# A state-space block and six layers of local attention and FFN: rounded output product, keys placed by transfer, Gelu from PSUM, new orders

## The chip, the cores and the metric

The kernel runs on one core of one Trainium2 chip. The metric is the device time of one execution in microseconds, median of three: 3040.13 us before the change (3039.28 to 3040.23). PE is TensorE, DVE is VectorE, ACT is ScalarE, POOL is GpSimd, SP is SyncE.

## The reference

Input x has 128 sequences of 32 tokens of 128 features. First comes a state-space block: input projection, a causal convolution of four taps, silu, a layer norm, and over the 32 tokens in order a recurrence of a state of 16 rows by 256 channels for each sequence, clipped to +/-10 at each step; the result is gated and projected back to 128 features.

```python
def step(h, inputs):
    ad, bd, xt, ct = inputs
    h = jnp.clip(h * ad[:, :, None] + bd[:, :, None] * xt[:, None, :], -10.0, 10.0)
    yt = jnp.einsum('bd,bdh->bh', ct, h)
    return (h, yt)
```

Then come six layers. Each shifts half of the features by one token, forms q, k, v (16 heads of 64) by a product of 128 by 3072, normalises and rotates q and k, attends with a causal mask within a window of 32 tokens (here one sequence), and adds the output product (1024 by 128) to the residual. An FFN follows: a token shift, layer norm, a product to two times 341, `a * gelu(gate)`, and a product back to 128, added to the residual. At the end x is added.

## The kernel before

Everything is written by hand: each engine has its own program, and semaphores order them. There are three parts.

**cond_block** handles the state-space block. A first loop over the 32 tokens convolves and normalises. In a second loop, the recurrence, ACT forms the outer products of the input with the state's coefficients in PSUM (outer), DVE updates state rows (recur, L518), POOL updates the rows below PS (side, one row) from ACT's product side_u, DVE clips all 16 rows (clip, L528), and PE sums the rows with diagonal matrices (y_product, L239) that POOL writes (diagonals, L436). PE's project first puts the bias into PSUM by a product with ones (L207). POOL's side waits for the clip of the step before, PE's y_product for the clip of its own step.

**stack** handles the six layers. Each layer has 32 tiles of 128 tokens in 8 groups of four, so there are 192 tiles and 48 groups in all. A body(i, l, g) on every engine has four steps j. In step j the engines work on tiles of several ages: tile n is projected, tile n-1 is transposed (transpose_q, transpose_k at L803, copy_qT, copy_kT), tile n-2 has its scores and exponentials, tile n-3 its values (weigh_values L855) and its output copy (copy_oT L1028). The order of calls within body is each engine's order of work and nothing else sets it. Layer 0's groups 0 and 1 are unrolled, the others of it, and all eight of each later layer, are in hardware loops (group_steps).

The projection (L775) is three rounded (float32r) passes for each half of 512 columns: w_hi with xs_hi, w_lo with xs_hi, w_hi with xs_lo, where hi is the rounded value and lo the rest. Each layer's weights come in eight parts (load_part on SP, into a w_part of two buffers), which ACT rounds (round_part, L1099) and POOL completes (rest_of_part, L1335) during the layer before. The two PSUM tiles pa hold q, k and v in turn. ACT squares q and k, DVE sums the squares (L1161) and multiplies by sines (L1177) and cosines (L1168), and POOL adds the two (rotate, L1312) and scales the keys (norm_keys, L1321). project_v waits for DVE's cosines of q, and the next project_q for those of k. The keys are copied on ACT in two pieces of 64 partitions (L1011) into the layout of kT, block by block. Probabilities are transposed by DVE (L1186) and placed into pT by four DMAs on SP's queue. The values' result px is copied to oT, which has two buffers by group:

```python
if k == 0:
    wait_for(act, s["wo_done"], g - 1)
act.copy(oT[:, bass.ds(g % 2, 1), :, k, :]...
```

The output product project_out (L868) is one fp32 product of 512 columns for each of eight head pairs, 16 instructions, in j=3 of the body behind the group, half before transpose_k and half after. add_attention (DVE, L1233) adds it to res. The FFN runs in the body after that: centre (L1070) and variance in j=0, normalise (DVE, L1226), scale_shift (ACT, L1091), three gate products (L894) in j=1 with a bias copy each (gate_bias, L1036), then one Gelu over all (L1043) between two table loads; three a products (L905), gated (L1218), and down (L912) in j=2.

**add_input** transposes the residual and adds x.

Of the kernel before, what the change touches and what calls it, by code (L numbers as in the profile page):

```python
# [15 lines left out]
F32 = mybir.dt.float32  # L16
# [6 lines left out]
P = 128  # L23
# [3 lines left out]
PS = 1  # L27
# [22 lines left out]
EXP_LN = "natural_log_exp_and_others"  # L50

# [11 lines left out]
def cond_block(nc, d, res, spare, w0_loaded):  # L63
    with ExitStack() as ctx:
# [3 lines left out]
        def sem(name):  # L68
# [19 lines left out]
        wx, wxdt = room[0:NPROJ, 6656:6912], room[0:DS, 6912:7168]  # L88
        ident = sb("c_ident", [P, P])
# [5 lines left out]
        ones = sb("c_ones", [P, P])  # L95
        dt_bias = sb("c_dt_bias", [32, NPROJ])
# [24 lines left out]
        side_u = sb("c_side_u", [P, 2, PS, DI])  # L121
# [6 lines left out]
        names = """win_loaded taps_loaded ln_loaded late_loaded bias_loaded zeroed winT_done winT_ready taps_ready tap_mul  # L128
            tap_bias_ready late_done late_ready var_ready x_transposed xT_ready conv_done gate_done pre_ready silu_done gate_ready
            stats_done aggr_done rstd_ready centred xn_ready sq_done clamped scale_ready dx_ready neg_a_tanh neg_a_ready  # L130
            xnT_done xnT_ready proj_done bc_ready dtt_ready decay_mul decay_ready side_u_ready side_mul side_ready
# [5 lines left out]
        with nc.Block() as block:  # L137
            @block.sync
            def _(sp):
                sp.dma_start(ident[:], d["ident"]).then_inc(s["win_loaded"], 16)  # L140
                sp.dma_start(win, d["W_in"].rearrange("(r p) m -> p r m", p=P)).then_inc(s["win_loaded"], 16)
                for k in range(S // XCHUNK):
# [6 lines left out]
                sp.wait_ge(s["zeroed"], 7)  # L149
                sp.dma_start(dt_bias[0:1, 2 * DS:NPROJ], d["b_dt"].rearrange("(o n) -> o n", o=1))\  # L150
                    .then_inc(s["bias_loaded"], 16)
# [6 lines left out]
            def _(pe):  # L158
# [42 lines left out]
                def project(t):  # L201
                    if t < S:
                        if t == 0:
                            pe.wait_ge(s["bias_loaded"], 16)
                        wait_for(pe, s["bc_ready"], t)
                        wait_for(pe, s["dtt_ready"], t)
                        pe.matmul(pproj[:, 0:NPROJ], ones[0:32, :], dt_bias[:], start=True, stop=False)  # L207
                        pe.wait_ge(s["xnT_ready"], t + 1)
                        for f in range(2):
                            last = pe.matmul(pproj[:, 0:NPROJ], xnT[:, f, :], proj_w[:, f, :], start=False, stop=(f == 1))  # L210
# [59 lines left out]
            def _(act):  # L270
# [6 lines left out]
                for tile, name, n in ((lng, "ln_g", DI), (lnb, "ln_b", DI), (dskip, "D", DI), (alog[:], "A_log", DS)):  # L277
                    act.dma_start(tile, row(name).to_broadcast([P, n])).then_inc(s["ln_loaded"], 16)
# [23 lines left out]
                def late_copies():  # L302
# [7 lines left out]
                    act.wait_ge(s["ln_loaded"], 4 * 16)  # L310
# [8 lines left out]
                def tanh_dt(t):  # L319
                    if t < S:  # L320
                        act.wait_ge(s["proj_done"], t + 1)
                        wait_for(act, s["decay_mul"], t - 1)
                        act.activation(dtt[:, t % 2, :], pproj[:, 2 * DS:NPROJ], ACT.Tanh).then_inc(s["dtt_ready"], 1)
# [38 lines left out]
                for t in range(S):  # L362
# [6 lines left out]
                    if t >= S - 3:  # L369
                        k = t - (S - 3)  # L370
                        copy_xnT(k)
                        if k:
                            tanh_dt(k - 1)
                square(S - 2)
                square(S - 1)
                side_outer(0)
                outer(0, 0, 2)
                for t in range(S + 3):
                    outer(t, 2, NPAIR)
# [1117 lines left out]
```

## Time and profile before

| what | value |
|---|---|
| median of three runs | 3040.13 us |
| the profiled execution | 3038.72 us |
| its span, first to last instruction | 3036.9 us |
| mean granted TensorE clock | 0.985 |
| PE busy, share of the span | 2893.9 us, 95% |
| DVE busy | 2400.4 us, 79% |
| ACT busy | 2425.5 us, 80% |
| POOL busy | 2079.6 us, 68% |
| recurrence | about 95 to 404 us |
| layers | about 408 to 3019 us |

In a timeline a row gives the start of an instruction, its duration, its engine, line, operation and tiles. Neighbours on one engine overlap by a little, so the distance of two starts is what an instruction takes from its queue, and its duration is what its follower on another engine sees. PE's ends are modelled.

### The profile page before, as it was taken

How to read it: one execution, taken by the hardware profiler on the slowest of the kernel's cores; microseconds unless marked ns; L12 is line 12 of the kernel's file. 1: busy time of each engine (PE TensorE's matmuls, PEld its weight loads, DVE VectorE, ACT ScalarE, POOL GpSimd, SP SyncE). 2: the span in 40 equal slices, each digit the busy share in tenths (PEclk: the TensorE clock that was granted, in tenths of full speed). 3: DMA queues.
4: the chain of work that ended last, by engine and by line, in shares of the span. 5: the costliest groups of instructions: out<-in, count | busy, mean ns of one | idle time of the engine just before them, and what ended most of it. 6: DMA issues, size and time to landing. Idle time of an engine off the chain costs nothing. (4 is left out here: it accounts for less than half of the span.)

```text
span 3036.9 us, 90328 instructions
## 1 busy us (share of the span) xinstructions
PE 2893.9 (95%) x35040; PEld 2002.2 (66%) x35040; DVE 2400.4 (79%) x3168; ACT 2425.5 (80%) x3783; POOL 2079.6 (68%) x1518
## 2 busy tenths in 40 slices
PE   8799978999999999999999999999999999999996
PEld 7688856666666666666666666666666666666662
DVE  7899967888788878778887787887788787888871
ACT  5788857888788888878788887878888887888872
POOL 6655557777777777677777677777777776776760
PEclk9899989999999999999999999999999999999997
DMA  1000011010011001010100110010110101100002
GB/s 51 22 1 1 1 28 29 23 26 23 23 32 34 23 20 26 24 38 23 26 23 22 33 31 25 21 26 24 28 33 23 26 23 26 28 21 21 18 20 64
DMA packets 72899, 76.58 MB, mean 25 GB/s; under 512 B 22937, under 2 KB 46551, under 8 KB 72663
## 3 DMA queue, kind: packets, MB, share of 16 engines
q1 hardware_dynamic: 71782, 74.01, 9.5%
q10 hardware_dynamic: 1008, 1.19, 0.2%
q8 instruction: 61, 1.00, 0.1%
q14 instruction: 48, 0.39, 0.0%
HBM read 22.71 MB, written 2.10 MB: 8 GB/s over the span
## 5 line engine op out<-in xcount | busy, mean ns | idle before, releaser
L1312 POOL TENSOR_TENSOR qk_r<-qk_r,qk_t 128x1024 f32<-128x1024 f32 x384 | 917.3, 2389 | 552.3 <-DVE qk_r L1168 388.0
L775 PE MATMUL pa<-w_hi,xs_hi 128*128 128x512 f32 x1152 | 577.1, 501 | 43.1 <-DVE qk_r L1168 26.1
L1161 DVE TENSOR_REDUCE ss<-sq 128x16 f32<-128x1024 f32 x384 | 463.5, 1207 | 18.7 <-ACT sq L958 18.4
L1177 DVE TENSOR_TENSOR qk_t<-pa,rot 128x1024 f32<-128x1024 f32 x384 | 465.4, 1212 | 0.0
L1168 DVE TENSOR_TENSOR qk_r<-pa,rot 128x1024 f32<-128x1024 f32 x384 | 465.3, 1212 | 0.0
L803 PEld LDWEIGHTS px<-ident_sb,qk_r 128*128 128x128 f32 x3072 | 350.9, 141 | 164.7 <-issue 100.4
L775 PE MATMUL pa<-w_hi,xs_lo 128*128 128x512 f32 x1152 | 455.8, 396 | 0.0
L775 PE MATMUL pa<-w_lo,xs_hi 128*128 128x512 f32 x1152 | 454.3, 394 | 0.0
L803 PE MATMUL px<-ident_sb,qk_r 128*128 128x128 f32 x3072 | 401.4, 274 | 30.7 <-POOL qk_r L1321 14.9
L1011 ACT COPY kT<-px 64x1024 f32<-64x1024 f32 x384 | 385.1, 1003 | 35.7 <-PE px L803 31.0
L1321 POOL TENSOR_TENSOR qk_r<-qk_r,inv 128x1024 f32<-128x1024 f32 x192 | 365.6, 1904 | 44.4 <-ACT inv L995 44.3
L775 PEld LDWEIGHTS pa<-w_hi,xs_hi 128*128 128x128 f32 x1152 | 217.6, 189 | 224.0 <-issue 178.0
L1186 DVE STREAM_TRANSPOSE prT<-pr 128x512 f32<-128x512 f32 x192 | 136.6, 711 | 265.6 <-POOL pr L1343 262.8
L868 PE MATMUL pg<-spare,wo 128*128 (+1 forms) x768 | 345.4, 592 | 1.1 <-ACT spare L1028 1.1
L965 ACT ACTIVATE sq<-pa 128x1024 f32<-128x1024 f32 x192 | 196.3, 1022 | 170.3 <-DVE ss L1161 160.3
L1028 ACT COPY spare<-px 128x1024 f32 (+1 forms) x192 | 193.2, 1006 | 108.9 <-PE px L855 107.8
L775 PEld LDWEIGHTS pa<-w_lo,xs_hi 128*128 128x128 f32 x1152 | 219.0, 190 | 78.3 <-issue 52.3
L775 PEld LDWEIGHTS pa<-w_hi,xs_lo 128*128 128x128 f32 x1152 | 217.7, 189 | 50.6 <-issue 0.2
L1343 POOL TENSOR_TENSOR pr<-pr,rden 128x512 f32<-128x512 f32 x192 | 201.8, 1051 | 66.6 <-DVE rden L1209 66.6
L239 PE MATMUL c_bank<-c_h,c_cdiag 128*128 128x256 f32 x1024 | 230.7, 384 | 10.9 <-DVE c_h L528 10.8
L868 PEld LDWEIGHTS pg<-spare,wo 128*128 128x128 f32 x768 | 141.9, 190 | 143.7 <-issue 138.4
L342 ACT ACTIVATE c_bank<-c_xn,c_bc 128x256 f32<-128x256 f32 x480 | 203.3, 468 | 38.4 <-DVE c_bc L504 24.2
(145 smaller groups left out, 5431.0 us busy)
## 6 DMA issues: line engine op xcount, KB each, us to landing
pT<-prT SPq DMA_DIRECT2D x768, 64.0 KB, 2.0
w_part<-in_Wqkv SPq DMA_DIRECT2D x40, 192.0 KB, 2.6
wo<-in_Wo SPq DMA_DIRECT2D x6, 512.0 KB, 4.1
c_h<-in_x SPq DMA_DIRECT2D x4, 512.0 KB, 9.0
o_x<-in_x SPq DMA_DIRECT2D x8, 256.0 KB, 5.1
out<-o_out SPq DMA_DIRECT2D x8, 256.0 KB, 4.3
w<-in_W SPq DMA_DIRECT2D x6, 341.0 KB
spare<-in_Wqkv SPq DMA_DIRECT2D x1, 1536.0 KB, 6.3
```

The lines of the kernel that those rows point to most:

```text
L239: last = pe.matmul(py[t % 2][:, 0:DI], cdiag[:, t % 3, n, :], h[:, t % 2, n, :], start=False, stop=(n == DS - 1))
L342: last = act.activation(pu[k % 2][:, (n - lo) * DI:(n - lo + 1) * DI], xn[:, t, :], ACT.Copy, scale=bc[:, t % 2, 0, n:n + 1])
L775: last = pe.matmul(pa[(u + c) % 2][:, half * 512:half * 512 + 512], x[:, j * P:(j + 1) * P], w[:, at], start=(k == 0), stop=(k == 2))
L803: last = pe.transpose(px[:, hp * P:(hp + 1) * P], qk_r[:, j % 2, c, hp * P:(hp + 1) * P], ident[:])
L868: last = pe.matmul(pg[:], wo[:, hp, :], heads_out, start=(hp == 0), stop=(hp == HP - 1))
L1011: act.copy(kT[rows, :, :, half, :].rearrange("p h b j -> p (h b) j"), px[rows, :].rearrange("p (h j) -> p h j", j=S)).then_inc(s["tk_out"], 1)
L1161: dve.reduce_sum(ss[:, c, :], heads(sq[:]), AX.X).then_inc(s[sum_sem], 1)
L1168: dve.tensor_tensor(heads(qk_r[:, j % 2, c, :]), heads(pa[(3 * j + c) % 2][:]), per_head(rot[:, l % 2, 2 * c, :]), ALU.mult).then_inc(s[co ...
L1177: dve.tensor_tensor(halves(qk_t[:, c, :]), halves(pa[(3 * j + c) % 2][:])[:, :, ::-1, :], table.unsqueeze(1).to_broadcast([P, HEADS, 2, DH ...
L1312: pool.tensor_tensor(qk_r[:, j % 2, c, :], qk_r[:, j % 2, c, :], qk_t[:, c, :], ALU.add)\
L1321: pool.tensor_tensor(k_r, k_r, over(inv[:, j % 2, 1, :], DH), ALU.mult).then_inc(s["norm_k"], 1)
L1343: pool.tensor_tensor(keys(pr[:]), keys(pr[:]), over(rden[:], S), ALU.mult)\
```

## The change

In cond_block:
- PS is 2: POOL updates two state rows, DVE 14 in seven pairs.
- The bias product on PE goes; DVE adds the bias from a tile (dt_in) in scale_bc, and tanh_dt reads that tile. tanh_dt has a new place on ACT.
- Two skip terms and the last clipped_norm move on POOL to behind the second step.

In stack:
- The output product has three rounded passes per head pair, 24 in all, from wo_hi, wo_lo, oT_hi, oT_lo. ACT rounds wo (round_wo) and POOL completes it (rest_of_wo), once a layer, at g == 1, j == 0. ACT's copy writes oT_hi, and a new DVE subtraction, rest_of_outputs, writes oT_lo from px. Both have one buffer, not two.
- project_out is split: its first half in j=3 of body i, its second in j=0 of body i+1, behind project_q. add_attention and shift_ffn move to j=0.
- The keys are copied in one piece into k_both, and two DMAs on SP's queue place it in kT (place_keys).
- Gelu is applied in the copies from PSUM (gate_gelu), with the table loaded before copy_qT of j=1. scale_shift is a tensor_scalar on DVE.
- w_part has one buffer; round_part moves to j=0. v and qk_r lie in spare.
- floor_norms, log_norms and inverse_norms of a tile move to the next step; every engine's order is new.
- Groups 0 and 1 of every layer are unrolled. PE's waits at its start move to the first transpose.

```diff
-PS = 1
+PS = 2
...
                     if t < S:
-                        if t == 0:
-                            pe.wait_ge(s["bias_loaded"], 16)
                         wait_for(pe, s["bc_ready"], t)
-                        wait_for(pe, s["dtt_ready"], t)
-                        pe.matmul(pproj[:, 0:NPROJ], ones[0:32, :], dt_bias[:], start=True, stop=False)
+                        wait_for(pe, s["dt_ready"], t)
...
-                        dve.wait_ge(s["dtt_ready"], t + 1)
+                        dve.wait_ge(s["proj_done"], t + 1)
+                        wait_for(dve, s["dtt_ready"], t - 1)
+                        dve.tensor_tensor(dt_in[:, t % 2, :], pproj[:, 2 * DS:NPROJ], bdt[:], ALU.add)\
+                            .then_inc(s["dt_ready"], 1)
...
-        oT = spare[:].rearrange("p (g h t n) -> p g h t n", g=2, h=HP, t=GT)
+        oT_hi = sb("oT_hi", [P, HP, GT, P], F32R)
+        oT_lo = sb("oT_lo", [P, HP, GT, P], F32R)
...
+                def place_keys(i, j, back):
+                    n, _, live = tile(i, j, back)
+                    if live:
+                        sp.wait_ge(s["tk_out"], n + 1)
+                        wait_for(sp, s["scores_done"], n)
+                        for half in range(2):
+                            rows = slice(half * DH, (half + 1) * DH)
+                            sp.dma_start(kT[rows, half].rearrange("p h b j -> p (h b j)"), k_both[rows, :])\
+                                .then_inc(s["kT_ready"], 16)
...
                         for hp in range(lo, hi):
-                            heads_out = oT[:, bass.ds(g % 2, 1), hp, :, :].rearrange("p o t n -> p (o t n)")
-                            last = pe.matmul(pg[:], wo[:, hp, :], heads_out, start=(hp == 0), stop=(hp == HP - 1))
+                            for k, (w, o) in enumerate(((wo_hi, oT_hi), (wo_hi, oT_lo), (wo_lo, oT_hi))):
+                                last = pe.matmul(pg[:], w[:, hp, :], o[:, hp, :, :].rearrange("p t n -> p (t n)"),
+                                                 start=(hp == 0 and k == 0), stop=(hp == HP - 1 and k == 2))
...
                         if k == 0:
-                            wait_for(act, s["wo_done"], g - 1)
-                        act.copy(oT[:, bass.ds(g % 2, 1), :, k, :].rearrange("p o h (r q) -> p (o r) h q", r=2),
+                            wait_for(act, s["wo_done"], i + (j - back) // GT)
+                        act.copy(oT_hi[:, :, k, :].rearrange("p h (r q) -> p r h q", r=2),
...
+                        dve.tensor_scalar(fx[:], fx[:], ln_par[:, 0:1], ln_par[:, 1:2], ALU.mult, ALU.add)\
+                            .then_inc(s["fn_ready"], 1)
...
+                        dve.tensor_tensor(oT_lo[:, :, k, :].rearrange("p h (r q) -> p r h q", r=2),
+                                          px[:].rearrange("p (r h q) -> p r h q", r=2, h=HP),
+                                          oT_hi[:, :, k, :].rearrange("p h (r q) -> p r h q", r=2).bitcast(F32), ALU.subtract)\
+                            .then_inc(s["oT_lo_ready"], 1)
```

The new order of a body on PE, ACT, DVE and POOL, as the change has it (the number is the age of the tile, or of the group):

```
PE    [j2 a_block 0] project_q [j2 a_block 1] [j0 project_out second half] scores 2, transpose_q 1, [j2 a_block 2]
      [j1 gate 0] project_k [j0 subtract_mean] [j3 project_out first half] transpose_k 1, [j2 down] [j1 gate 1]
      project_v [j1 gate 2] mask 1, weigh_values 3, [j0 variance]
ACT   [round_wo once a layer] floor 1, [j1 inverse_deviation] log 1, [j0 round_part, shift_hi] square_q, inverse 1,
      [j0 shift_ffn] [j1 table] copy_qT 1, [j2 shift_hi] [j1 gelu 0] square_k [j0 copy_centred] [j1 gelu 1] copy_kT 1,
      [j0 square_centred] [j1 gelu 2] copy_v, copy_oT 3, [j1 table] [j0 log_variance] exponentials 2
DVE   [j3 add_ffn] [j1 normalise, scale_shift] [j2 gated 1] [j0 add_attention] sin_q, turn_probs 3, [j2 gated 2]
      sum_q, cos_q, maximum 2, sin_k, cos_k, subtract 2, sum_k, [j1 gated 0] rest_of_outputs 3, denominators 2
POOL  norm_scores 3, rotate_k 1, [j3 shift_lo] norm_probs 3, norm_keys 1, [j3 rest_of_part] rotate_q,
      [j1 shift_lo] [rest_of_wo once a layer]
```

## Rows read from the trace of the kernel before

**Rows 1.** The page, part 1: busy time of each engine in the whole span

```profile
PE 2893.9 (95%) x35040; PEld 2002.2 (66%) x35040; DVE 2400.4 (79%) x3168; ACT 2425.5 (80%) x3783; POOL 2079.6 (68%) x1518
```

**Rows 2.** Timeline of DVE (start us, us): normalise in four groups

```profile
787.24 0.69 DVE L1226 TENSOR_TENSOR fn<-fc,pg 128x512 f32<-128x512 f32 x1 [0.31 <-ACT pg L1084]
...
843.04 0.68 DVE L1226 TENSOR_TENSOR fn<-fc,pg 128x512 f32<-128x512 f32 x1
...
1478.33 0.69 DVE L1226 TENSOR_TENSOR fn<-fc,pg 128x512 f32<-128x512 f32 x1 [0.29 <-ACT pg L1084]
...
1530.88 0.69 DVE L1226 TENSOR_TENSOR fn<-fc,pg 128x512 f32<-128x512 f32 x1 [0.30 <-ACT pg L1084]
```

**Rows 3.** Timeline of PE (start us, us) inside one group

```profile
1513.29 3.60 PE L868 MATMUL pg<-spare,wo 128*128 x8
...
1520.78 0.50 PE L775 MATMUL pa<-w_hi,xs_hi 128*128 128x512 f32 x1
...
1522.27 1.04 PE L803 MATMUL px<-ident_sb,qk_r 128*128 128x128 f32 x8
1523.14 1.02 PE L877 MATMUL pg<-fs,center_sb 128*128 128x512 f32 x2
...
1528.79 0.39 PE L824 MATMUL ps<-mask_b,ident_b 128*128 128x512 bf16 x1
...
1530.20 1.10 PE L834 MATMUL ps<-kT,qT 128*32 128x64 f32 x64
1531.23 0.50 PE L775 MATMUL pa<-w_hi,xs_hi 128*128 128x512 f32 x1
```

**Rows 4.** Timeline of DVE in the same group

```profile
1522.52 0.71 DVE L1186 STREAM_TRANSPOSE prT<-pr 128x512 f32<-128x512 f32 x1 [0.92 <-POOL pr L1343]
...
1523.73 1.20 DVE L1161 TENSOR_REDUCE ss<-sq 128x16 f32<-128x1024 f32 x1
1524.85 1.21 DVE L1177 TENSOR_TENSOR qk_t<-pa,rot 128x1024 f32<-128x1024 f32 x1
```

**Rows 5.** Timeline of ACT in the same group

```profile
1519.45 0.39 ACT L1054 CAST xs_hi<-res 64x256 fp32r x1
...
1520.29 1.01 ACT L1028 COPY spare<-px 128x1024 f32 x1
1521.32 0.32 ACT L987 ACTIVATE ln_ss<-over_floor,floor_c 128x32 f32<-128x32 f32 x1
...
1540.81 1.28 ACT L1043 ACT_TABLE_LOAD   x1
```

**Rows 6.** The page, part 6: issues, KB each, median us to landing

```profile
pT<-prT SPq DMA_DIRECT2D x768, 64.0 KB, 2.0
...
wo<-in_Wo SPq DMA_DIRECT2D x6, 512.0 KB, 4.1
```

**Rows 7.** Timeline of SP's queue (start us, us)

```profile
1510.27 2.41 SPq L745 DMA_DIRECT2D pT<-prT  x4
```

**Rows 8.** Timelines of PE, DVE and POOL in one step of the recurrence

```profile
236.13 0.42 PE L207 MATMUL c_bank<-c_dt_bias,c_ones 32*128 32x48 f32 x2
...
235.96 2.29 DVE L528 TENSOR_SCALAR c_h<-c_h 128x4096 f32<-128x4096 f32 x1
...
239.38 5.88 DVE L518 SCALAR_TENSOR_TENSOR c_h<-c_h,c_decay,c_bank 128x256 f32<-128x256 f32 x13
245.30 2.29 DVE L528 TENSOR_SCALAR c_h<-c_h 128x4096 f32<-128x4096 f32 x1
...
239.08 0.73 POOL L418 TENSOR_TENSOR c_h<-c_h,c_side_u 128x256 f32<-128x256 f32 x1
...
240.24 3.61 POOL L436 TENSOR_TENSOR c_cdiag<-c_ident,c_bc 128x2048 f32<-128x2048 f32 x1
```

**Rows 9.** L528 alone: duration ns min/median/max, first and last start

```profile
L528 DVE TENSOR_SCALAR c_h<-c_h x32: 2293/2293/5714, 101.2 to 394.6; 128x4096 f32<-128x4096 f32 x32
```

More of the change, by code:

```diff
@@ L662, in group_steps @@
         def group_steps(eng, body, new_layer):
-            new_layer(0)
-            body(0, 0, 0)
-            body(1, 0, 1)
-            with eng.Fori(2, GROUPS) as g:
-                body(g, 0, g)
-            for l in range(1, DEPTH):
+            for l in range(DEPTH):
                 new_layer(l)
-                with eng.Fori(0, GROUPS) as g:
+                for g in range(2):
+                    body(g + l * GROUPS, l, g)
+                with eng.Fori(2, GROUPS) as g:
                     body(g + l * GROUPS, l, g)
@@ L1035, in gate_bias, with tables, shift_hi @@
                         act.wait_ge(s["gate_done"], 3 * g + k + 1)
-                        act.activation(gt[0:m, k, :], pg[0:m, :], ACT.Identity, bias=b1[0:m, 1, k:k + 1])\
+                        act.activation(gt[0:m, k, :], pg[0:m, :], ACT.Gelu, bias=b1[0:m, 1, k:k + 1])\
                             .then_inc(s["gate_out"], 1)
-                def gelu(i):
-                    g, live = group(i, 2)
+                def tables(i, back, name):
+                    g, live = group(i, back)
                     if live:
-                        act.wait_ge(s["gate_out"], 3 * g + 3)
-                        act.activation(gt[:], gt[:], ACT.Gelu).then_inc(s["gelu_done"], 1)
-                        act.preload_act_table_set(EXP_LN)
-                def shift_hi(i, back, half):
+                        act.preload_act_table_set(name)
+                def shift_hi(i, back, half, first=False):
                     g, live = group(i, back)
+                    live = live and (first or not isinstance(g, int) or g > 0)
                     if live:
@@ L1076, in log_variance, with inverse_deviation @@
                     if live:
                         act.wait_ge(s["var_done"], g + 1)
[L1078 to L1081 removed]
+                        act.activation(fx[:], pg[:], ACT.Ln, bias=eps_c[:]).then_inc(s["fln_done"], 1)
+                def inverse_deviation(i, back):
+                    g, live = group(i, back)
                     if live:
@@ L1094, in round_part, with round_wo @@
+                def round_wo(l):
+                    act.wait_ge(s["wo_loaded"], 16 * (l + 1))
+                    wait_for(act, s["wo_done"], l * GROUPS)
+                    act.copy(wo_hi[:], wo[:]).then_inc(s["wo_hi_ready"], 1)
                 def round_part(l, g):
@@ L1128, in body @@
[L1128 to L1139 removed]
+                            gate_gelu(i, 2, 1)
@@ new lines, in body @@
+                        copy_kT(i, j, 1)
+                        if j == 0:
+                            square_centred(i, 2)
+                        if j == 1:
+                            gate_gelu(i, 2, 2)
+                        copy_v(i, j, 0)
+                        copy_oT(i, j, 3)
+                        if j == 1:
+                            tables(i, 2, EXP_LN)
+                        if j == 0:
+                            log_variance(i, 2)
+                        exponentials(i, j, 2)
@@ L1290, in _, with shift_lo @@
             def _(pool):
-                def shift_lo(i, back, half):
+                def shift_lo(i, back, half, first=False):
                     g, live = group(i, back)
+                    live = live and (first or not isinstance(g, int) or g > 0)
                     if live:
@@ L1305, in shift_lo, with rotate @@
                         pool.wait_ge(s["xs_ready"], 2 * chunk + 2)
-                def rotate(i, j, c, cos, sin, rotated):
-                    n, j, live = tile(i, j, 1)
+                def rotate(i, j, back, c, cos, sin, rotated):
+                    n, j, live = tile(i, j, back)
                     if live:
```

512 lines of the change are left out of this document (257 added, 255 removed).

## The prediction

> **What bounds the kernel now.** I read the page first: PE is busy 95% of the span, DVE, ACT and POOL 68 to 80% [rows 1]. That is an average, so next comes the period. DVE's normalise (L1226) runs once per group; two neighbours in mid-layer lie 52.55 us apart, and two across a layer's end 55.80 us [rows 2]. There are 48 groups of four tiles, so one microsecond per group is 48 us. Third, the spacing of PE's work inside a group [rows 3]: a projection (six passes) takes 1.49 us, eight transposes 0.87, the mask with the value products 1.41, the scores 1.03. Eight of the sixteen output instructions are 3.60 busy, of which some 0.25 overlaps their follower: 3.35 a half. The two instructions of one fp32 product (L877) are 1.02 busy, likewise 0.87. Twelve projections, eight transpose sets, four value and four score sets, two output halves and eleven fp32 products make 17.9 + 7.0 + 5.6 + 4.1 + 6.7 + 9.6 = 50.9 of 52.55 us. **PE bounds the layers**, and waits take 1.65 us per group. In the recurrence of the first block a step takes 9.34 us (clip to clip), and PE and DVE are both dense [rows 8].
>
> **Part 1, output product.** 16 fp32 instructions become 24 rounded passes. A projection shows six such passes in 1.49 us [rows 3], so 24 take 5.6 us against 6.7: PE gains 1.1 us per group, and its dense sum falls to 49.8.
> New on DVE: a subtraction per tile (px minus oT_hi, 128x1024, source PSUM as in L1177), 1.13 us from start to start (L1161 to L1177 is 1.12, busy 1.21) [rows 4], 4.5 per group. ACT loses work: keys are copied in one piece, the separate Gelu pass and the scale and shift go.
>
> **The wait that this adds.** oT was double by group; oT_hi and oT_lo are single. copy_oT of a group's first tile stands on ACT in j=3 of body i and waits for wo_done of the previous group. The second half of that product stands on PE in body i+1, j=0, behind project_q. Behind the waiting copy on ACT lie the exponentials, floor, log, round_part, two shifts and square_q; behind square_q on DVE lie sin_q and all that follows; behind those PE's project_v. The chain from the start of project_q, hops of 0.1 to 0.2 us included: project_q 1.49, output half 2.8, hop 0.2; copy 0.9 (1.01 as the row has it, the next starts earlier), exponentials 0.55 (half a copy's elements), floor and log 0.55 (two of 0.32, overlapped), round_part and two shifts 1.25 (two casts start 0.84 before the copy behind them), square 1.0 [rows 5]; this makes 8.8. DVE: sin 1.13, transpose 0.63 (0.71 busy), sum 1.12, cos 1.13 = 4.0 [rows 4]; 12.8. PE: hop, project_v, mask and values, one fp32 product: 0.2 + 1.49 + 1.41 + 0.87 = 4.0. Step j=0 takes 16.8 us, while PE's own work in it is 8.65 (a plain tile: three projections, two transpose sets, values, scores) + 2.8 + 1.74 = 13.2. So 3.6 us of PE idle.
>
> **The other steps**, with the same durations. j=1: PE 8.65, three gate products and the first a product 3.5 = 12.1. PE could start the first gate product 3.4 us into the step (project_q, scores, transposes). But after variance ACT has logarithm, exponentials, floor and inverse_deviation, some 2.2 us into the step, and DVE then normalise and scale_shift: ready at 4.0 to 4.4. ACT, with two table loads of 1.28 [rows 5], three Gelus, three copies and two squares, is nearly full too: 13.1, one us of it waiting. j=2: PE 13.0, no wait of size. j=3: PE 8.65 + 2.8 = 11.5, no wait. Sum 16.8 + 13.1 + 13.0 + 11.5 = 54.4; as the scale's wait (below) is uncertain by 0.4, I take **54.2 us**, 1.65 over now. Of 48 groups 46 run at this period (the first two have no full pipeline): +76 us.
>
> **Keys by transfer.** Two issues of 0.6 us (four of pT take 2.41 [rows 7]) and a landing: 64 KB land in 2.0 us, 512 KB in 4.1 [rows 6]; the pair, 512 KB, is nearest the second, so kT is there some 4 us after the copy. The scores of that tile stand behind the next project_q, some 4 us later: cost nothing, bound +1 per group. pT is ready 3.9 us behind its transpose (its fourth issue begins at 1.8); the values come 3.9 or more behind it: nothing, but no cover is left. The single w_part lands behind the keys, but round_part has the wait for wo_done as cover; if that cover goes, 0 to 0.5 per group.
>
> **Scale and shift on DVE.** ACT's op leaves, a tensor_scalar arrives. The clip (L528), a tensor_scalar from SBUF to SBUF, took 2.29 us in the middle and 5.71 at most [rows 9]; what is over is 3.42, about one of POOL's diagonals ops of 3.61 [rows 8]. norm_probs is the POOL op that the new one meets; POOL's add of 256 columns takes 0.73 [rows 8], and norm_probs has twice the columns. So the meeting costs 0 to 0.75 per group; below 0 is out, as no op gets shorter. I took half. The Trainium skill, SBUF — State Buffer, Who interferes with whom, says the one that starts first gets the shared port for its whole instruction and the other fully blocks; the maximum row agrees. By that rule alone the period would be 54.4 rather than 54.2, and the time 3093 us.
>
> **Layer ends.** Now 3.25 us extra at each [rows 2], five of them: POOL's tables stand before the rotation that PE waits for. In the new order they stand before norm_scores, which has slack behind the ACT wait: -16 us. **Rounding wo**: a 128x1024 copy on ACT, right in the j=0 chain (0.9), and a subtraction on POOL (at most 2.9, four times the add of 256 columns [rows 8]; 1.3 of it late for the scores): 2.2 x 6 = +13 us. More unrolled bodies: nothing, as the first two groups of layer 0 show no fetch stalls of size; bound 0 to +2 per layer.
>
> **The recurrence.** PE loses the bias product, 0.42 us busy, 0.35 to its follower; DVE loses one of 13 rows in 5.88 us (0.45) and gains a small add (0.1) [rows 8]. Both fall by 0.33 to 0.35 per step of 9.34: 32 x 0.33 = -11 us. POOL's second row costs at most what its first does, the add 0.73 and a multiply below that, say 1.1 in all; diagonals end at 243.85, the clip starts at 245.30 [rows 8], 1.45 apart, less 0.35: they just do not meet. If they meet, the clip waits, and the gain falls to -5. The first clip starts behind deferred POOL work: -1.
>
> **Ends.** The stack's first product no longer waits for the masks, memsets and the other thirds of the weights: 0 to -4, taken as -3 (three DVE ops of the 1.2 us kind [rows 4] leave the front of it). Filling the first two groups, with shorter ACT work: 0 to -20, taken as -10. The drain saves a table load and part of the Gelu: -4.
> Sum: 76 - 16 + 13 - 11 - 1 - 3 - 10 - 4 = **+44 us**. The profiled execution took 3038.72 us (span 3036.9), 1.4 under the median of 3040.13; so 3038.7 + 44 + 1.4 = 3084 us.
>
> **Rivals.** (a) *The wait is absorbed and PE stays the bound.* For it: PE is dense today, and ACT and DVE lose or move work. Against it: wo_done is a program dependency that no slack on ACT removes. At 50.9 a group (49.8 with 1.1 of waits): -1.65 x 46 = -76, with the rest -32: 2932 us. In between lies the point at 53.25, where 0.70 x 46 cancels the 32 and the time stays as it is. Chance of the faster side 0.21.
> (b) *No difference*: my walk is 1.0 too long in each group, 53.1 to 53.4: 3034 to 3046. Chance 0.06.
> (c) *Forecast*: 53.4 to 55, most of it over 53.7, chance 0.60. For it: in-order queues, and each hop of the chain is a wait in the code with a duration from a row. Against it: PE's dense sum leaves 4.4 us of room that another order of arrivals could use.
> (d) *Transfers late or PE slowed*: keys and pT have no cover; one us late each group adds 46, or idle of several us drops the granted clock: 3130 and over. Chance 0.13.
> (e) *The rounding is no gain*: were the new passes as long as the fp32 instructions, 24 for 16 would add 3.3 us a group. Against it: the projection's passes [rows 3]. Within (d).
>
> **How the numbers follow.** Likeliest 3084 us. The slope is 46 us per us of period. The forecast's own range is 53.7 to 55: 3061 to 3121. Down to 3005 takes in waits partly absorbed (52.5), up to 3130 a late transfer; about 1 in 10 lies beyond each end. Faster by over 0.2% (about what a measurement of this kernel can tell from no change): 0.21; within 0.2%: 0.06; slower: 0.73.
>
> **What would show it.** In the new profile: L1226's group spacing near 54.2; ACT idle of about 4 us once per group before the copy to oT_hi, ended by PE's output product; PE idle in three pieces of j=0 that sum to 3 to 4 us; 24 output passes 0.23 apart; recurrence steps of 9.0; layer ends without the extra 3 us; scale_shift's longest duration over 0.35 us if it met POOL. Wrong if the spacing is under 53, or if PE's waits end on kT or pT transfers.

## Result and profile after

The changed kernel takes **3355.68 us** (median of 4 runs, 3354.37 to 3357.79); the kernel before took 3040.18 us beside it (3039.28 to 3040.64). The ratio is 1.104, with a 95% interval of 1.102 to 1.106. Slower was forecast, but 3084 us, and the range ended at 3130: the direction was right, and the size was missed by 272 us.

The page of the changed kernel, part 1, and its rows of part 6 (issues, KB each, median us to landing):

```profile
PE 2836.3 (85%) x35168; PEld 2089.6 (62%) x35360; DVE 2634.6 (79%) x3407; ACT 2156.9 (64%) x3499; POOL 2138.8 (64%) x1523
...
kT<-k_both SPq DMA_DIRECT2D x384, 256.0 KB, 3.6
pT<-prT SPq DMA_DIRECT2D x768, 64.0 KB, 2.0
w_part<-in_Wqkv SPq DMA_DIRECT2D x40, 192.0 KB, 3.7
wo<-in_Wo SPq DMA_DIRECT2D x6, 512.0 KB, 5.8
```

The span grows by 319 us and no engine is busier than PE's 85%: no engine took over as the bound, and PE waits. PE's 58 us less than before [rows 1] is no saving. Its row has 35168 instructions and that of its weight loads 35360: the 192 records of the mask's product (L843) are missing from PE's row in this trace. In runs that have them the values start 0.30 to 0.32 us behind the mask, so the missing records stand for some 60 us in all. The pace is in DVE's timeline, by the normalise (now L1245):

```profile
1482.77 0.63 DVE L1245 TENSOR_TENSOR fx<-fc,pg 128x512 f32<-128x512 f32 x1
1543.03 0.63 DVE L1245 TENSOR_TENSOR fx<-fc,pg 128x512 f32<-128x512 f32 x1
1602.28 0.63 DVE L1245 TENSOR_TENSOR fx<-fc,pg 128x512 f32<-128x512 f32 x1
1662.64 0.63 DVE L1245 TENSOR_TENSOR fx<-fc,pg 128x512 f32<-128x512 f32 x1
```

The three gaps are 60.26, 59.25 and 60.36, and the 45 full gaps between groups average 59.9 us, against 52.55 [rows 2] and the 54.2 forecast. The 5.7 us over the forecast, times 46 groups, are 262 of the 272 us missed. The miss is one of the period. Where the period went stands in the chain of waits by group (line waited for: us in total, times, longest):

```profile
DVE oT_lo L1259 <- ACT oT_hi L1045: 466.3, 145, 7.9
...
ACT oT_hi L1045 <- PE pg L886: 301.8, 47, 8.1
PE px L873 <- DVE sm L1219: 269.2, 184, 2.2
ACT oT_hi L1045 <- PE px L873: 215.6, 145, 9.4
...
ACT sq L983 <- DVE ss L1181: 202.2, 189, 3.1
...
PE px L819 <- DVE oT_lo L1259: 66.2, 47, 1.5
PE pg L896 <- ACT fs L664: 54.6, 48, 2.1
...
PE pg L914 <- DVE fx L1252: 12.3, 31, 2.9
```

The second row is the wait that was forecast: ACT idles for 6.4 us per group there, where some 4 were forecast. Of PE's own waits the largest is the third, **for the subtraction of the maximum, in four pieces per group**, and the prediction doesn't have it. The row says 5.6 us per group; as it takes in the missing mask products, some 0.31 each, what is left is about 4.4 (an estimate), 212 us in all. The timelines of one group show both. ACT and DVE from the copy that waits for the output product:

```profile
1525.32 1.01 ACT L1045 CAST oT_hi<-px 128x1024 fp32r<-128x1024 f32 x1 [6.49 <-PE pg L886]
...
1528.58 1.03 ACT L976 ACTIVATE sq<-pa 128x1024 f32<-128x1024 f32 x1
```

```profile
1529.64 1.22 DVE L1197 TENSOR_TENSOR qk_t<-pa,rot 128x1024 f32<-128x1024 f32 x1
...
1532.51 1.21 DVE L1188 TENSOR_TENSOR spare<-pa,rot 128x1024 f32<-128x1024 f32 x1
1533.64 0.68 DVE L1212 TENSOR_REDUCE top<-ps 128x16 f32<-128x512 f32 x1
1534.23 1.21 DVE L1197 TENSOR_TENSOR qk_t<-pa,rot 128x1024 f32<-128x1024 f32 x1
1535.37 1.21 DVE L1188 TENSOR_TENSOR spare<-pa,rot 128x1024 f32<-128x1024 f32 x1
1536.50 0.68 DVE L1219 TENSOR_TENSOR sm<-ps,top 128x512 f32<-128x512 f32 x1
```

PE in the same stretch (in brackets the idle time before a row and what ended it):

```profile
1519.41 1.16 PE L873 MATMUL px<-pT,spare 64*64 64x64 f32 x64 [1.62 <-DVE sm L1219]
1520.84 0.47 PE L791 MATMUL pa<-w_hi,xs_hi 128*128 128x512 f32 x1 [0.27 <-issue]
...
1522.31 0.40 PE L886 MATMUL pg<-oT_hi,wo_hi 128*128 128x512 f32 x1
1522.54 0.40 PE L886 MATMUL pg<-oT_lo,wo_hi 128*128 128x512 f32 x1
...
1527.65 1.09 PE L819 MATMUL px<-ident_sb,spare 128*128 128x128 f32 x8 [1.39 <-DVE oT_lo L1259]
...
1533.86 0.47 PE L791 MATMUL pa<-w_hi,xs_hi 128*128 128x512 f32 x1 [0.53 <-DVE spare L1188]
...
1537.63 1.24 PE L873 MATMUL px<-pT,spare 64*64 64x64 f32 x64 [2.14 <-DVE sm L1219]
1538.79 2.07 PE L903 MATMUL pg<-fx,mean_sb 128*128 128x512 f32 x2
1539.88 1.42 PE L791 MATMUL pa<-w_hi,xs_hi 128*128 128x512 f32 x1
```

The maximum starts at 1533.64; the keys' two rotation products (L1197, L1188) stand between it and the subtraction, which starts at 1536.50. The mask overwrites the scores that it reads, so PE's mask, and the values (L873) queued behind it, start when it ends. It ends at 1537.18, and the mask's weight load starts at 1537.29. The pieces are 1.62 (j=3), 2.14 (j=0), 1.28 (j=1) and 0.79 (j=2): 5.8 us, some 4.6 of it without the masks.

### The profile page after: what moved, and what is told of

Read it like the earlier page. It is cut to its first block and busy times, and to the rows that moved or that the text cites. A ratio compares the mean times of both kernels' runs of the same rounds, so it can differ in the third digit from the quotient of the medians.

```text
span 3356.0 us, 90298 instructions
## 1 busy us (share of the span) xinstructions
PE 2836.3 (85%) x35168; PEld 2089.6 (62%) x35360; DVE 2634.6 (79%) x3407; ACT 2156.9 (64%) x3499; POOL 2138.8 (64%) x1523
## 5 line engine op out<-in xcount | busy, mean ns | idle before, releaser
L1348 POOL TENSOR_TENSOR spare<-spare,qk_t 128x1024 f32<-128x1024 f32 x384 | 917.1, 2389 | 351.4 <-DVE spare L1188 351.4
L1259 DVE TENSOR_TENSOR oT_lo<-px,oT_hi 128x1024 fp32r<-128x1024 f32 x192 | 234.7, 1222 | 466.3 <-ACT oT_hi L1045 466.3
L1045 ACT CAST oT_hi<-px 128x1024 fp32r<-128x1024 f32 x192 | 194.7, 1014 | 517.4 <-PE pg L886 301.8
L1197 DVE TENSOR_TENSOR qk_t<-pa,rot 128x1024 f32<-128x1024 f32 x384 | 465.8, 1213 | 25.8 <-ACT sq L976 22.5
L819 PE MATMUL px<-ident_sb,spare 128*128 128x128 f32 x3072 | 411.6, 277 | 72.2 <-DVE oT_lo L1259 66.2
L873 PE MATMUL px<-pT,spare 64*64 64x64 f32 x12288 | 231.4, 226 | 277.3 <-DVE sm L1219 269.2
L1188 DVE TENSOR_TENSOR spare<-pa,rot 128x1024 f32<-128x1024 f32 x384 | 464.1, 1209 | 0.0
L819 PEld LDWEIGHTS px<-ident_sb,spare 128*128 128x128 f32 x3072 | 341.5, 141 | 150.9 <-DVE oT_lo L1259 55.7
L1357 POOL TENSOR_TENSOR spare<-spare,inv 128x1024 f32<-128x1024 f32 x192 | 368.8, 1921 | 32.8 <-ACT inv L1015 29.8
L1364 POOL TENSOR_TENSOR sm<-sm,inv 128x512 f32<-128x512 f32 x192 | 201.5, 1050 | 140.6 <-DVE sm L1219 136.9
L990 ACT COPY spare<-pa 128x1024 f32<-128x1024 f32 x192 | 193.7, 1009 | 127.6 <-PE pa L791 127.5
```

The lines of the kernel that those rows point to most:

```text
L819: last = pe.transpose(px[:, hp * P:(hp + 1) * P], qk_r[:, j % 2, c, hp * P:(hp + 1) * P], ident[:])
L873: last = pe.matmul(px[at:at + DH, to:to + 64], v[rows, j, h * DH:(h + 1) * DH], pT[rows, :, h, :], start=True, stop=True, skip_group_check ...
L1188: dve.tensor_tensor(heads(qk_r[:, j % 2, c, :]), heads(pa[(3 * j + c) % 2][:]), per_head(rot[:, l % 2, 2 * c, :]), ALU.mult).then_inc(s[co ...
L1197: dve.tensor_tensor(halves(qk_t[:, c, :]), halves(pa[(3 * j + c) % 2][:])[:, :, ::-1, :], table.unsqueeze(1).to_broadcast([P, HEADS, 2, DH ...
L1259: dve.tensor_tensor(oT_lo[:, :, k, :].rearrange("p h (r q) -> p r h q", r=2), px[:].rearrange("p (r h q) -> p r h q", r=2, h=HP), oT_hi[:, ...
L1348: pool.tensor_tensor(qk_r[:, j % 2, c, :], qk_r[:, j % 2, c, :], qk_t[:, c, :], ALU.add)\
```

## Experiments

In the times below a single time is one run; kernels timed in rounds have their interval. In the diffs, lines are of the changed kernel unless said otherwise.

**The first block alone.** The kernel before with the changed first block (b_dt added on DVE, two state rows on POOL), its stack as it was.

> The kernel before with the first block of the changed one (two state rows on POOL, bias added by DVE). Its own theory: the first block ends 13 to 14 us earlier, as in the changed kernel's trace, so 3027 us, 3024 to 3030. Rival: POOL's longer work meets the clip in some steps and the gain is under 6 us: 3034 or more.

Measured: 3028.32 us, ratio 0.995 (0.994 to 0.997). The first block gives some 14 us back, so the changes to the stack cost 327. It is the base for the orders of before below; its groups in mid-layer are 52.5 us apart.

**The subtraction behind the maximum.**

```
                         maximum(i, j, 2)
+                        subtract_maximum(i, j, 2)
                         times_sin(i, j, l, 1, "sq_k", "rot_k", "sin_k")
                         times_cos(i, j, l, 1, "sq_k", "tk_done", "cos_k")
-                        subtract_maximum(i, j, 2)
```

> From the changed kernel, one call of DVE moved: the maximum's subtraction (which frees ps for the mask, and with it PE's mask and value products) comes right behind the maximum, ahead of the keys' sines and cosines. Theory A (the prediction's walk missed the mask's wait, 269 us in all; with it gone the loop has the walk's period of about 54.5 us instead of 59.9): 3100 us, between 3070 and 3140, and PE's wait of the value products for the subtraction nearly gone. Theory B (all of the loss is ACT's wait for the output product, 302 us): 3300 us or more. Theory C (the loss is the lower granted clock): 3250 us or more, with the clock still under 0.98.

Measured: **3120.3 us, 235 less**. Waits by group:

```profile
ACT oT_hi L1045 <- PE pg L886: 237.9, 47, 5.3
...
PE px L819 <- DVE oT_lo L1259: 65.7, 47, 1.5
```

PE's wait for the subtraction is gone from the list, the copy's wait for the output product is still there, and the spacing is 54.5 us, 0.3 from the forecast of 54.2. One line moved on DVE settles three quarters of the loss. Theories B (3300 or more) and C (3250 or more, for the clock) fell; the mean granted clock rose with it, from 0.97 to 0.983. A part of the 235 came back by it: the variance instruction takes 655 ns on average instead of 893, which for 96 of them is 23 us.

**The output product's second half back in j=3.**

```
-                        if j == 0:
-                            project_out(i, 2, HP // 2, HP)
...
                         transpose_k(i, j, 1)
+                        if j == 3:
+                            project_out(i, 1, HP // 2, HP)
```

> From the changed kernel, the second half of the output product moved on PE from the next body's j=0 back to j=3, behind the keys' transposes, so that ACT's copy no longer waits for the next body. Theory A (two waits, each with its own price; this one some 3.6 us a group): 3180 us, 3150 to 3220, with the mask's wait of PE still there, 250 us or more. Theory B (this wait is all of the loss): 2930 to 3000 us.

Measured: 3217.1 us, 139 less, spacings in mid-layer 55.9 to 57.5; PE's wait for the subtraction stays, with 151.2 us instead of the 250 expected (now on the mask's own row, so to be held against the 212 above). So the forecast wait is real and costs 3.0 us a group here, against 3.6 forecast.

**Both.**

> Both moves together: subtraction early, output product whole in j=3. Theory A: the two prices add, period 51 to 52 us, 2970 us, 2930 to 3010, faster than the kernel before. Theory B: as the output move alone. A third theory, that DVE's new subtraction from px and the transfers hold the loop: 3080 us or more.

Measured: 3046.8 us, spacing 52.4. The two gains, 235 and 139, sum to 374, and together they give 309: they share some 65 us, and behind the moved subtraction the output product's place is worth only 74 us, 1.6 a group. All three expectations were missed: 2970 us was too low, and neither 3217 nor 3080 and more came. What is left against the base of 3028 is 19 us, although PE's own work is less by 1.1 us a group. PE's largest waits are then these:

```profile
PE pg L896 <- ACT fs L664: 54.8, 48, 4.2
PE pa L791 <- DVE spare L1188: 20.2, 38, 1.5
PE ps L853 <- DMA kT<-k_both: 17.8, 28, 2.7
PE pg L914 <- DVE fx L1252: 17.0, 41, 2.9
```

The 19 us don't lie in the period: in mid-layer the groups are 52.4 us apart, in the base 52.5. They lie where a layer begins. The groups there are 57.0 and 56.1 us apart at the first layer's end, 56.0 and 57.7 at the next. Summed over each layer end, what its gaps have over those in mid-layer is 9.2, 9.2, 8.1, 9.0 and 2.9 us, 38 in all, and in the base 4.2, 4.6, 4.1, 4.1 and 2.0, 19 in all. In the second of these groups SP's queue issues the next part of the weights behind the transfers of the FFN's weights, ACT's rounding waits for it, and PE waits for the copies to fs that stand behind it on ACT (SP, ACT, PE):

```profile
1353.82 0.43 SPq L703 DMA_DIRECT2D w_part<-in_Wqkv  x1
```

```profile
1356.44 0.51 ACT L1118 CAST w_hi<-w_part 128x384 f32 x1 [3.32 <-DMA w_part<-in_Wqkv]
```

```profile
1360.25 2.08 PE L896 MATMUL pg<-fs,center_sb 128*128 128x512 f32 x2 [4.24 <-ACT fs L664]
```

In the first of them ACT waits 1.12 us for wo and rounds it in 1.05, and PE's wait for fs is 3.04. The wait for fs in the list above is therefore no 1.1 us in every group: it is about 0.55 us in most groups and 2.0 to 4.2 in nine at the layers' beginnings, which have 30 of the 54.8. The wait for w_part comes at four of the five layer ends, 3.1 to 3.3 us each, and once at the stack's start; the fifth end, where no part is left to load, is the one with 2.9. The kernel before has two buffers for w_part, and no ACT wait for it.

**The addition and the copies to fs in j=3** (in the kernel with both).

```
-                        if j == 0:
-                            add_attention(i, 2)
...
+                        if j == 3:
+                            add_attention(i, 1)
                         rest_of_outputs(i, j, 3)
...
+                        if j == 3:
+                            shift_ffn(i, 1)
                         copy_v(i, j, 0)
```

> The changed kernel with the subtraction behind the maximum, the whole output product in j=3, and now also the addition to the residual and the copies to fs in j=3. In the kernel without this last step (3046.8 us) PE waited 1.35 us per group for fs. Theory A (that wait is the largest that is left, and nothing stands behind it): spacing 51.3, 1.1 us x 46 less, about 2997 us (2985 to 3015). Rival B (the two copies to fs now stand ahead of the copy of the values and push ACT's chain in j=0 by as much): 3035 to 3060.

Measured: 3112.41 us, 66 more: both expectations missed, the rival in its size. ACT now waits for the addition, 3.6 us per group, ahead of the copy of the values, and PE's transposes wait for the keys that POOL normalises late. The waits:

```profile
ACT fs L1079 <- DVE res L1269: 171.8, 48, 10.2
...
PE px L819 <- POOL spare L1357: 74.3, 52, 3.8
```

An op moved to where its engine seemed idle took its unfinished operand along.

**ACT's rounding and shift in j=0 moved behind the copy of the outputs** (the same base).

> The changed kernel with the subtraction behind the maximum and the whole output product in j=3 (3046.8 us as it is), and with the rounding of the next weights' part and the second half of the input's shift moved on ACT, in j=0, from ahead of square_q to behind the copy of the outputs: the 1.25 us of three casts leave the front of ACT's j=0. Theory A (PE's 1.35 us per group ended by the copies to fs are ACT's density at the front of j=0): spacing 51.5, about 3000 us (2990 to 3015). Rival B (PE's wait there comes from the values and project_v, and returns in the next step, as with the residual moved to j=3): 3035 to 3060.

Measured: 3051.95 us. The wait for fs falls from 54.8 to 28.2, and the one for scale and shift (L914) rises from 17.0 to 55.2: the wait moved one product on. Rival B. The sum hides two changes: ACT no longer waits for w_part, and the layer ends cost 8 us in all instead of 38; but in mid-layer the groups are 53.2 us apart instead of 52.4.

**The keys again by two copies on ACT** (the same base).

```
-                        wait_for(act, s["kT_ready"], 32 * n)
-                        act.copy(k_both[:], px[:]).then_inc(s["tk_out"], 1)
+                        wait_for(act, s["scores_done"], n)
+                        for half in range(2):
+                            rows = slice(half * DH, (half + 1) * DH)
+                            act.copy(kT[rows, half].rearrange("p h b j -> p (h b j)"), px[rows, :]).then_inc(s["tk_out"], 1)
```

> The changed kernel with the subtraction behind the maximum and the whole output product in j=3 (3046.8 us), its keys again placed by two copies of 1.0 us on ACT and not by one copy and two transfers. Theory A (the transfers are nearly hidden: 17.8 us of PE's waits in all end on them, and ACT's second copy costs 1.0 us per tile, of which j=0 and j=1 are dense): 3050 to 3095 us. Rival B (the transfers' landing is what is left of the loss against the order of before): 3025 to 3035. No difference within 5 us means that the way the keys go doesn't matter.

Measured: 3067.31 us (1.009, 1.008 to 1.011): 20 more than with transfers, with 87.5 us of PE's waits at the values ended by this copy (the mask's records are missing here too, some 0.31 in each of the 95). Theory A. In mid-layer the groups are 53.5 us apart, 1.1 more, while the layer ends cost 10.5 us in all instead of 38. So the transfers help the period of this order and make the layer ends dearer; that they are no part of what is left is not shown.

**The rounded output product in the order of before.** 24 passes, oT_hi and oT_lo, wo rounded once a layer, groups 0 and 1 of every layer unrolled, the whole product in j=3, and on DVE:

```
                         denominators(i, j)
...
+                        rest_of_outputs(i, j)
                         maximum(i, j)
```

> The order of before with the new first block, and of the change to the stack only the output product: 24 rounded passes, the subtraction per tile on DVE, the single oT_hi and oT_lo (the whole product stays in j=3, ahead of the copy that waits for it), wo rounded on ACT and POOL once per layer. Theory A (PE bounds the layers of before, so what its product loses shows): 1.1 us less of PE per group, 48 groups, less some 6 us for the rounding of wo, 3028 falls to about 2980 (2970 to 3000), group spacing 51.4. Rival B (the subtraction stands ahead of the queries' transposes and of the maximum on DVE, and its wait takes back what PE gains): 3028 or above, spacing 52.5 or more, PE's waits at the transposes ended by oT_lo.

Measured: 3063.47 us (1.008, 1.006 to 1.010), 35 over the base, spacing 53.25: rival B. PE's record:

```profile
PE px L803 <- DVE oT_lo L1239: 82.2, 94, 2.1
```

PE's work shrank, and the queries' transposes wait for the subtraction that the rounding needs. **In this order the product's 1.1 us don't show as time.**

**Gelu from PSUM, with the rounded product and without.**

```
                         if j == 1:
-                            gate_bias(i, 0)
+                            tables(i, GELU)
+                            gate_gelu(i, 0)
...
-                            gate_bias(i, 2)
-                            gelu(i)
+                            gate_gelu(i, 2)
+                            tables(i, EXP_LN)
```

> The same with Gelu straight from PSUM in three pieces, the table loaded ahead of the first gate product, and no separate Gelu pass. ACT loses about 1.3 us per group. Theory A (ACT is off the path, and PE's first a product stands a tile behind the gate products): within 8 us of the kernel without it. Rival B (in j=1 ACT is nearly full and its table load delays the copy that the key transposes need): 20 to 50 us longer, with PE idle in j=1 ended by ACT. Third possibility, a gain: 10 to 30 us less, if ACT's pass held the exponentials back.

> The order of before with the new first block and Gelu from PSUM in three pieces with early tables, the output product in fp32. Theory A (PE is the bound here at a spacing of 52.58 with 410 of 420 us busy, and ACT has slack): within 5 us of the kernel without it, 3023 to 3033; the 30 us that Gelu gave beside the rounded product were ACT reaching the copy of the outputs earlier. Rival B (ACT holds PE up in fp32 as well): 3000 to 3015.

Measured: 3033.01 us with it (0.998, 0.997 to 0.999), **30 less**; and in fp32, without the rounded product, 3050.53 us (1.004, 1.002 to 1.005), **22 more** than the base. The same edit has two signs. In both, PE waits for the first Gelu, which stands behind the table load. With the rounded product:

```profile
PE pg L896 <- ACT gt L1037: 51.0, 49, 2.1
...
PE px L804 <- DVE oT_lo L1240: 17.1, 46, 2.1
```

There ACT reaches the copy of the outputs earlier, and the 82.2 us for oT_lo fall to 17.1. In fp32 there is no such wait to shorten, and 57.1 us of the new one are added. For fp32 I had expected no change or a gain. With Gelu from PSUM on both sides the rounded product is 17 us faster than the fp32 one (3033.01 against 3050.53, in two series of runs), and the groups in mid-layer are 52.6 us apart against 53.1: half of its 1.1 us does show there.

**POOL's tables inside the layer's first group, in halves.** With the rounded product and Gelu (wo's subtraction in halves too), and in fp32 with Gelu (groups 0 and 1 of every layer unrolled too).

```
                         norm_scores(i, j)
+                        if isinstance(g, int) and g == 0 and l + 1 < DEPTH and j in (0, 2):
+                            rotary_tables(l + 1, (j // 2,))
```

> The order of before with the new first block, rounded output product and Gelu from PSUM (3033.0 us), POOL's tables now in two halves inside the first group of a layer instead of in one piece ahead of the layer, and the subtraction for wo in two halves. Layer ends stand out by 3.0 us and the third group by 2.0 in that kernel: 5 x 3.0 + 3 x 1.5 = 20 less, about 3014 us (3008 to 3022) if POOL's queue ahead of the rotation makes them. If the wait is for something else at a layer's start: no change, 3030 to 3036.

> The order of before with the new first block, output product in fp32, Gelu from PSUM, and POOL's tables in two halves inside the first group of a layer. Layer ends lose their 3.25 us x 5 = 16: about 3010 us (3004 to 3018). If the wait is for something else at a layer's start: 3023 to 3033.

Measured: **3016.68 us (0.993, 0.991 to 0.994)** and 3032.70 us (0.998, 0.997 to 0.999), 16 and 18 less. The spacing across a layer's end falls from 55.6 to 52.6 in the first, from 56.5 to 53.1 in the second. In fp32 the step came as expected and the time didn't: 3010 had been added up from the 3028 of the kernel without Gelu. The first is 16 us faster than the second, again by the rounded product. It is faster than both kernels of this study and the fastest of all here.

**Scale and shift on DVE, in that kernel**, as tensor_scalar, and then as scalar_tensor_tensor with the shift as a broadcast operand.

> The fastest kernel so far (3016.7 us: the order of before, new first block, rounded output product, Gelu from PSUM, tables and wo in halves), with the scale and shift of the normalised rows on DVE (0.76) instead of ACT (0.81). In it ACT has no idle time from the start of j=0 to the end of j=1, and PE waits 1.07 us per group for the first Gelu. Theory A (ACT's dense stretch sets that wait): 0.8 us less per group, 48 groups, about 2980 us (2972 to 2995). Rival B (the op on DVE stands ahead of the subtraction that the queries' transposes wait for, 0.76 later): 3010 to 3030.

> The kernel with the scale and shift on DVE (3031.1 us), the same arithmetic now as scalar_tensor_tensor with the shift as a broadcast tensor operand and not as tensor_scalar. There tensor_scalar took 1.82 us in the median, and ended 0.28 us behind POOL's addition of the rotation, which runs when it starts. Theory A (tensor_scalar waits for POOL's running instruction, a form with two tensor operands doesn't, like DVE's multiplications beside the same POOL op): its row 0.75 or below, spacing 53.0 falls by 0.4 to 1.1, 2980 to 3012 us. Rival B (any DVE op here is slowed by POOL, or the time is the broadcast's or the two pointers' own): its row over 1.2 us, 3025 to 3035.

Measured: 3031.08 us (0.997, 0.996 to 0.998) and 3067.79 us (1.010, 1.008 to 1.012): 14 and 51 more than with the op on ACT, so neither gain came; the first is 1 us over rival B's range, the second 33 over its own rival's. The op alone in each (duration min/median/max in ns):

```profile
L1231 DVE TENSOR_SCALAR fn<-fn,ln_par x48: 547/1819/1839, 513.3 to 2988.9; 128x512 f32<-128x512 f32 x48
```

```profile
L1231 DVE SCALAR_TENSOR_TENSOR fn<-fn,ln_par x48: 750/2089/2112, 513.9 to 3024.4; 128x512 f32<-128x512 f32 x48
```

And beside POOL, in the tensor_scalar kernel, first DVE and then POOL:

```profile
1413.04 0.69 DVE L1224 TENSOR_TENSOR fn<-fc,pg 128x512 f32<-128x512 f32 x1 [0.15 <-ACT pg L1084]
1413.84 1.81 DVE L1231 TENSOR_SCALAR fn<-fn,ln_par 128x512 f32<-128x512 f32 x1
```

```profile
1412.97 2.40 POOL L1329 TENSOR_TENSOR spare<-spare,qk_t 128x1024 f32<-128x1024 f32 x1 [0.94 <-DVE qk_t L1175]
```

POOL's addition ends at 1415.37, DVE's op at 1415.65; the second form ends 0.55 behind such an addition. The same POOL op leaves the normalise (L1224) alone, 0.69 with one operand in PSUM. Both forms of the scale wait for POOL, so my theory A for the second form, that two tensor operands avoid it, fell. The op is 0.27 us longer in the second form, 13 us in 48 groups, and the kernel 37: 16 of its 45 full gaps are 54.5 to 55.1 us long and most of the others 53.2, and why is not shown. The Trainium skill, SBUF — State Buffer, Who interferes with whom, says that a DVE instruction with two SBUF inputs contends with a GpSimd instruction that reads SBUF, and that one with at most one SBUF input outside the two-port modes doesn't. The normalise and the second form agree. The same section counts tensor_scalar among the ops that can take both ports, and its row waits too; in which mode it ran no row shows (its shortest, 0.547 us for 512 elements of a partition, is about twice the clip's time per element, 2.29 for 4096 [rows 8]).

## Why the prediction was wrong, point by point

- **"The wait that this adds"** was right as far as the chain goes on ACT and DVE. From project_q at 1520.84, it gave the end of square_q 8.8 us later, and it ended at 1529.61 (8.77); DVE's part was to end at 12.8, and the next project_v started at 1533.86 (13.0). The second half of the product was costed at 2.8 us and the scores behind it started 2.85 after its first pass.
- **The step that failed** is the last link: "PE: hop, project_v, mask and values, one fp32 product: 0.2 + 1.49 + 1.41 + 0.87 = 4.0". By these terms the mask was due 1.49 us behind project_v's start at 1533.86 and the values 0.3 behind the mask, at 1535.67; they started at 1537.63, 2.0 us later, because the mask waits for the subtraction of the maximum, which the new DVE order puts behind both rotation products of the keys. In the kernel before it stood at the front of DVE's body, and the walk took the mask's place in the queue and forgot its wait. The prediction checked the added wait and not the old ones against the new order.
- **"The other steps"** have the same hole. From project_q to project_q: j=0 16.8 forecast, 19.0 measured; j=1 13.1, 14.2; j=2 13.0, 13.8; j=3 11.5, 13.2. With the subtraction moved up they are 16.6, 12.8, 13.2 and 11.9 and the spacing is 54.5: each step of the walk was right to 0.4 us once the missing wait is out. What the walk makes of the added wait was too much even so: without it the walk has 50.8, and 52.4 was measured, so it is worth 2.1 us of period there and not 3.6, as other waits for the same engines lie under it.
- **Output product**: passes 0.23 apart, as forecast. What was wrong is to count its 1.1 us as PE's gain whatever the order: in the order of before the rounded product costs 35 us, as DVE's subtraction holds the transposes, and with Gelu from PSUM it saves 16 to 17.
- **Keys by transfer**: 3.6 us to landing, 4 forecast, and with both waits removed they are 20 us cheaper than copies. The single w_part was priced at 0 to 0.5 per group if its cover went; with both waits removed ACT waits for it at four layer ends and at the stack's start, 15.7 us in all, and in no other group.
- **Scale and shift on DVE**: 0.76 us in the changed kernel, 0.21 more than the shortest of 0.55. That is the price of the meeting, within the forecast 0 to 0.75. It began while norm_probs ran on POOL and ended 0.3 us behind it. The mark for the meeting (over 0.35 us) told nothing, as the shortest is above it already.
- **The recurrence and the stack's start**: the stack's first product starts 14.3 us earlier (401.49 against 415.79), forecast 15; a step takes 8.94 us instead of 9.34, as forecast 9.0. The first block alone gives 14.
- **Layer ends** stand out no more, as forecast (-16), but by luck: the longer waits of every group covered them. With the subtraction moved up they cost 22 us in all, with both waits removed 38, in the kernel before 19.
- **Outside the period** the forecast had -32 us; 3355.7 less 3040.1 less 46 x 7.35 leaves -23, 9 us off in their sum. That is luck in part: with the subtraction moved up the same sum, 3120.3 less 3040.1 less 46 x 1.95, leaves -10. The filling, taken as -10, gained nothing: the stack starts 14.3 us earlier, and its first normalise only 1.2 (12.6 with the subtraction moved up).
- The rivals: none named this mechanism; (d) had the side of the range, for other reasons (transfers late, clock).
- **The signs**: PE's pieces in j=0 were to sum to 3 to 4 us; they are 1.39, 1.03 and 0.53, together 2.95.

What stays open: the 19 us between the kernel with both waits removed and the base. Its rows put them at the layers' beginnings, where ACT waits for w_part and wo, and not into the feed-forward part of every group; but no run gives w_part its second buffer back or moves its load ahead of the FFN's weights, so their price is not isolated. The three runs on this kernel (copies to fs, ACT's order in j=0, the keys' way) each made the period longer and the layer ends cheaper.

## What to carry to other kernels

When instructions are reordered on one engine, list every semaphore that the moved ones release, and look up who waits for it at the head of another queue: here an unchanged wait, four times per group, cost three quarters of the loss. A saving on the bounding engine is worth its time only if what it requires elsewhere (a rounding remainder, a table load) is ready before the bound engine's next wait: Gelu from PSUM gave -30 us beside the rounded product and +22 without it. Before a wait's total is spread evenly over the groups, look at the single gaps: here the rest of the loss sat in two groups of each layer. Before an elementwise op is moved to DVE, see what POOL runs at that moment and how many of its operands lie in SBUF.

## What the runs showed of the hardware that was not expected

DVE's scale of 128x512 took 0.55 us at the shortest and 1.82 in the median, behind a running POOL op that reads SBUF; as scalar_tensor_tensor 0.75 and 2.09. The form with more operands is longer on both counts. ACT does the same in 0.81.

The granted clock falls behind PE's waits. In the changed kernel's windows (PE, PEld, DVE, ACT, POOL busy, then the clock):

```profile
1535.00:1537.60 2.60, 0.49 (x3) 0.15 (x2) 2.60 (x4) 1.61 (x3) 1.60 (x2) 1.00 0.53 101
1537.60:1541.50 3.90, 3.87 (x68) 2.55 (x69) 1.93 (x2) 1.61 (x3) 3.01 (x2) 0.63 0.20 67
1541.50:1546.00 4.50, 4.50 (x81) 3.37 (x80) 3.72 (x6) 4.47 (x9) 2.74 (x2) 0.95 0.00 0
```

In the first stretch PE waited some 1.8 us (2.14 by the row, less the mask that the trace lacks); then the clock is 0.63, between the levels of 2.4 and 1.2 GHz, the two instructions of the variance product took 2.07 us where the kernel before needs 1.02 for such a pair [rows 3], and the next projection's first pass 1.42 instead of 0.50 [rows 3]. The mean duration of the variance instruction is 893 ns over the span against 605 before, so the wait in j=0 is paid a second time: 0.29 x 96 is 28 us in this line alone. With the subtraction moved up the mean is 655.
